# Turning gathered expert rows without TensorE: store, permuting loads and VectorE transposes, in a fused attention and mixture-of-experts kernel

## Chip, cores and metric

The kernel runs on one core of one Trainium2 chip. The metric is device time in microseconds (us). Before the change the median of 3 runs is 1353.02 us (1351.83 to 1355.73).

## The reference

The input x is 8 x 1024 rows of 256. Every row is layer-normalised; on the result xn two branches run, and the output is x + attention(xn) + experts(xn) + xn.

```python
Q, K, V = heads(xn @ Wq + bq), heads(xn @ Wk + bk), heads(xn @ Wv + bv)   # 16 heads of 16
Qp = relu(Q / |Q| @ projection) + 0.1          # 64 features per head; Kp the same from K
KV, K_sum = Kp^T V, sum over the sequence of Kp
out = (Qp KV) / max(Qp K_sum, 1e-6) @ Wo + bo

logits = xn @ router_w.T ; probs = softmax ; top 2 of 8 experts, weights renormalised
rank = position of the pair in its expert's list ; keep = rank < 2561
h = silu(rows of expert e @ w1[e])             # 256 -> 1024
y = h @ w2[e]                                  # 1024 -> 256
combined = sum over the two experts of weight * y
```

## The kernel before, in words

float32 products are made from float16 halves (high, low): each product is three matmul passes, high x high, high x low, low x high. `hl` in names means such a pair.

**Attention and routing.** Eight batches, each of 1024 rows in two halves of four 128-row tiles. A turn (`dve_turn`, `act_turn`, `pe_turn`, `pool_turn`, `sp_turn`) lists by hand, for each engine, its work on batch b and on the preparation of batch b+1, in order; engines meet by semaphores. Eight PSUM banks: four `big`, three `small` used in a ring, and a side bank. The steps that the change touches:
- `xn_high` (ScalarE) rounds half a batch of xn to float16, `x_low` (GpSimd, line 1038) takes the remainder, `x_transpose` (TensorE) turns both. `xhl` is also stored to DRAM as `xn_split`, 512 float16 per row (high 256, low 256).
- `q_relu` (ScalarE, line 522) and `q_low` (VectorE, 1369) split the query features; `kv_build` (VectorE) makes the kv matrix, with the cast of line 1360.
- The constant 0.1 of the features is handled apart. `constant_part` (VectorE, line 1378) writes norm x cn, for a 128-row tile 16 heads x 17 numbers, into `nd`; four tiles per half, so eight instructions per batch. `cn_b` is copied from PSUM by ScalarE. `attend_drain` (line 1385) adds the PSUM result of `attend` (TensorE, 823) to it.
- `norms` (VectorE) makes the norms of half 0, `norm_refine` (GpSimd) those of half 1.
- `place` finds each pair's slot, and `scatter` (GpSimd, line 1078) writes the batch's slot-table records to DRAM in 16 indirect DMAs. The batch before last still has 13 of them left when the tail begins; the last batch's 16 follow.

**Experts.** `tile_table` lists 71 tiles: the first 64 (`PT`) have 256 rows (two blocks of 128), the last 7 have one block, each tile of one expert. Per tile t:
- GpSimd: `meta_load` (1158) reads row numbers and weights of the tile, `gather` (1166) fetches its rows from `xn_split`, one indirect DMA per block, three tiles ahead (`XR` = 4 buffers, `xg`), `add_out` (1173) adds the result rows to the output in DRAM.
- TensorE: `hidden` (962) makes 1024 x rows in 48 matmuls, then `rows_turn` of tile t+1 (946: four transposes of 128 x 128 per block into bank 0 or 1), then `expert_out` of tile t-1 (979, 24 matmuls per block).
- VectorE: `hidden_split` splits silu(h) (1549, 1551, four times), then `rows_copy` of tile t+1 (1540) copies the turned rows from PSUM to `moe_xT`, then for the first 28 tiles `w_low` makes a low half of the next expert's weights (1263).
- ScalarE: silu (629), `w_high`, and `y_scale` (639).
- SP: in its order, for each tile, it waits for `rows_turned` and issues one `w_load` of 512 KB (tiles 1 to 26; line 410). Before the tiles it issued the output stores of the last batch.

The experts' SBUF area overlays attention's. VectorE therefore waits for the last output stores before its first `rows_copy` (line 1627).

## Time and profile before

| | |
|---|---|
| median of 3 runs | 1353.02 us (1351.83 to 1355.73) |
| profiled execution | 1353.69 us, span 1352.1 us |
| TensorE matmul (PE) busy | 1201.2 us, 89% |
| TensorE weight load (PEld) | 972.5 us, 72%, beside the matmuls |
| VectorE (DVE) | 870.9 us, 64% |
| GpSimd (POOL) | 679.7 us, 50% |
| ScalarE (ACT) | 621.4 us, 46% |
| `expert_out`, line 979 | 3240 matmuls, 365.3 us |
| `hidden`, line 962 | 3408 matmuls, 376.7 us |
| `rows_turn`, line 946 | 540 transposes |
| `rows_copy`, line 1540 | 71 copies, 0.68 us of a two-block tile |
| `constant_part`, line 1378 | 64 products, 433 ns |
| DMA | 80.64 MB, mean 60 GB/s |
| SP's DMA queue (q1) | 39330 packets, 9.5% of 16 engines |
| GpSimd's DMA queue (q0) | 32288 packets, 17.1% |

Shares are of the whole span, over two stages of very different kind: attention and routing until about 585 us, the experts after it. A matmul's busy time includes its latency, so that of single groups adds up to more than the time they occupy; the chain of waits gives the share of the path. "Idle before" is the time an engine did nothing before an instruction, with what released it; "issue" means that nothing in the profile shows a releaser. A DMA's "landing" is the time from its issue to its last byte.

### The profile page before, as it was taken

The numbers are of one execution on the slowest core, as the hardware profiler recorded it, in microseconds if no ns is written. First come the engines' busy times: TensorE is split into PE (matmuls) and PEld (weight loads), VectorE is DVE, ScalarE is ACT, GpSimd is POOL, SyncE is SP. The second block draws the span as 40 slices with busy tenths as digits, with TensorE's granted clock in tenths as the row PEclk, the third lists the DMA queues.
The fourth block names the chain that finished last, engine by engine and source line by source line (L and its number), as shares of the span: only waits on it lengthen the run. The fifth ranks groups of instructions, "written<-read, shape, count | busy, mean of one in ns | idle before, by whom it ended". The sixth has DMA issues, their size and how long they took to land.

```text
span 1352.1 us, 38635 instructions
## 1 busy us (share of the span) xinstructions
PE 1201.2 (89%) x14708; PEld 972.5 (72%) x14708; DVE 870.9 (64%) x2024; ACT 621.4 (46%) x1101; POOL 679.7 (50%) x646
## 2 busy tenths in 40 slices
PE   3779787878787888379999999999999999999997
PEld 1446464646564556259999999999999999989986
DVE  6778989898988886845555555554444444444442
ACT  3476767676757676333333333332222233233322
POOL 3313363636463637735555555555555555555542
PEclk9889798979888989589999999999999999999999
DMA  4111212112121111034444444433232332233330
GB/s 139 55 39 38 75 42 71 62 52 66 49 64 33 34 33 34 2 98 91 107 100 95 95 95 96 82 50 52 49 52 46 49 48 48 48 50 50 46 44 7
DMA packets 71788, 80.64 MB, mean 60 GB/s; under 512 B 14817, under 2 KB 65250, under 8 KB 71618
## 3 DMA queue, kind: packets, MB, share of 16 engines
q0 software_dynamic: 32288, 34.78, 17.1%
q1 hardware_dynamic: 39330, 43.39, 9.5%
q8 instruction: 131, 2.15, 0.7%
q14 instruction: 39, 0.32, 0.1%
HBM read 44.13 MB, written 34.92 MB: 58 GB/s over the span
## 4 chain that ended last, share of the span: by engine, by line
PE 66%; DVE 20%; issue 5%; ACT 4%; POOL 3%; DMA 1%; DVEq 0%; SPq 0%; ACTq 0%; POOLq 0%
PE bank L962 27%; PE bank L979 26%; DVE area L1369 4%; PE bank L703 2%; PE bank L823 2%; PE bank L946 2%; DVE area L1229 1%; PE bank L792 1%; DVE area L1378 1%; ACT area L502 1%; PE bank L809 1%; PE bank L764 1%; DVE area L1271 1%; DVE area L1360 1%; DVE area L1300 1%
## 5 line engine op out<-in xcount | busy, mean ns | idle before, releaser
L962 PE MATMUL bank<-area 128*128 128x256 f16 (+1 forms) x3408 | 376.7, 269 | 5.7 <-issue 3.1
L979 PE MATMUL bank<-area 128*128 x3240 | 365.3, 273 | 0.0
L962 PEld LDWEIGHTS bank<-area 128*128 x3408 | 324.7, 98 | 48.0 <-issue 7.8
L1549 DVE TENSOR_SCALAR area<-area 128x512 f16<-128x512 f32 (+1 forms) x284 | 125.3, 441 | 353.9 <-ACT area L629 350.7
L1173 POOL DMA_INDIRECT out_dram<-area,mt x135 | 218.4, 1618 | 247.4 <-ACT area L639 207.8
L979 PEld LDWEIGHTS bank<-area 128*128 128x128 f16 x3240 | 313.7, 98 | 35.6
L629 ACT ACTIVATE area<-bank 128x512 f32<-128x512 f32 (+1 forms) x284 | 163.7, 577 | 185.7 <-PE bank L962 184.2
L1078 POOL DMA_INDIRECT slot_table<-area x128 | 136.5, 1067 | 153.9 <-PE bank L823 96.7
L639 ACT ACTIVATE area<-bank,mt 128x256 f32<-128x256 f32 x135 | 57.1, 471 | 317.5 <-PE bank L979 317.5
L1551 DVE SCALAR_TENSOR_TENSOR area<-area 128x512 f16<-128x512 f32 (+1 forms) x284 | 189.5, 667 | 9.8
L1166 POOL DMA_INDIRECT xg<-xn_split,mt x135 | 135.4, 1003 | 42.6 <-issue 40.2
L703 PE MATMUL bank<-area,w_hl 128*128 128x512 f16 x384 | 91.5, 397 | 1.3 <-ACT area L540 1.3
L1158 POOL DMA_DIRECT2D mt<-slot_table x71 | 52.8, 743 | 77.3 <-issue 77.3
L522 ACT ACTIVATE area<-bank 128x512 f16<-128x512 f32 x128 | 67.4, 603 | 39.7 <-PE bank L809 19.8
L1369 DVE SCALAR_TENSOR_TENSOR area<-bank,area 128x512 f16<-128x512 f32 x128 | 79.6, 682 | 9.2 <-ACT area L522 8.4
L703 PEld LDWEIGHTS bank<-area,w_hl 128*128 128x128 f16 x384 | 38.1, 102 | 47.7 <-issue 9.8
L809 PE MATMUL bank<-area,p_hl 32*128 32x512 f16 x384 | 47.1, 429 | 27.8 <-DVE area L1369 24.6
L823 PEld LDWEIGHTS bank<-area 128*128 128x128 f16 x1536 | 44.2, 104 | 31.2 <-issue 23.8
L1038 POOL TENSOR_TENSOR area<-area 128x1024 f16<-128x1024 f32 x16 | 34.9, 2182 | 60.1 <-ACT area L534 60.1
L823 PE MATMUL bank<-area 128*128 128x34 f16 x1536 | 46.4, 188 | 20.7 <-issue 16.3
L728 PE MATMUL bank<-w_hl,area 128*128 128x264 f16 x384 | 51.8, 280 | 12.6 <-DVE area L1412 6.7
L728 PEld LDWEIGHTS bank<-w_hl,area 128*128 128x128 f16 x384 | 35.4, 99 | 37.4 <-DVE area L1412 14.2
(195 smaller groups left out, 1485.4 us busy)
## 6 DMA issues: line engine op xcount, KB each, us to landing
w_raw<-in_w_dram SPq DMA_DIRECT2D x18, 512.0 KB, 4.4
area<-in_x_dram SPq DMA_DIRECT2D x16, 512.0 KB, 5.9
xn_split<-area SPq DMA_DIRECT2D x16, 512.0 KB, 2.9
out_dram<-area SPq DMA_DIRECT2D x32, 256.0 KB, 3.5
area<-in_w_dram SPq DMA_DIRECT2D x14, 512.0 KB, 4.6
xg<-xn_split,mt POOLq DMA_INDIRECT x135, 3.4
out_dram<-area,mt POOLq DMA_INDIRECT x135, 3.9
slot_table<-area POOLq DMA_INDIRECT x128, 2.8
```

The source lines that it names most:

```text
L629: nc.scalar.activation(h32[j].rearrange("p a b -> p (a b)")[:, 0:n], big[j][:, 0:n], ACT.Silu, scale=1.0 / R_SCALE).then_inc(mh_silu, 1)
L703: mm = nc.tensor.matmul(big[n][:, :], w_hl[:, wl, k, c0:c0 + P], xT[half][:, xl * KC + k, :], start=(i == 0 and k == 0), stop=(i == 2 and ...
L728: mm = nc.tensor.matmul(dst[:, 0:D + E], xT[half][:, xl * KC + k, tl * P:(tl + 1) * P], w_hl[:, wl, k, 2 * D:], start=(i == 0 and k == 0), ...
L823: mm = nc.tensor.matmul(dst[:, p_ * KVW:(p_ + 1) * KVW], rq[:, p_, rl, tl * P:(tl + 1) * P], kv_hl[:, kl, p_, :], start=(i == 0), stop=(i ...
L962: mm = nc.tensor.matmul(big[j][:, i2 * n:(i2 + 1) * n], we[:, bass.ds(e * EXPERT + (k * 2048 + wl * 1024 + c * P), P)], moe_xT[t % XT][:, ...
L979: mm = nc.tensor.matmul(yb[:, a * D:(a + 1) * D], hT[u % 2][:, c, hl, a * P:(a + 1) * P], we[:, bass.ds(e * EXPERT + off, D)], start=(c == ...
L1078: nc.gpsimd.indirect_dma_start(meta, bass.IndirectOffsetOnAxis(slot_i[b % 2][:, k, t:t + 1], 0), rec[b % 2][:, k, t, :], None).then_inc(me ...
L1166: nc.gpsimd.indirect_dma_start(xg[:, t % XR, a, :], None, xs, bass.IndirectOffsetOnAxis(mt[:, u % GRP, a, 0:1], 0)).then_inc(rows_in[t % X ...
L1173: nc.gpsimd.indirect_dma_start(orows, bass.IndirectOffsetOnAxis(mt[:, u % GRP, a, 0:1], 0), y_sb[u % 2][:, a, :], None, bounds_check=last_ ...
L1369: v.scalar_tensor_tensor(rq[:, p_, 1, :], big[n % BIG_BANKS][:, :], 0.0, rq[:, p_, 0, :], ALU.max, ALU.subtract).then_inc(qf_split, 1)
L1549: v.tensor_scalar(hi, h, H_SCALE, None, ALU.mult).then_inc(mh_step, 1)
L1551: v.scalar_tensor_tensor(lo, h, H_SCALE, hi, ALU.mult, ALU.subtract).then_inc(mh_split, 1)
```

## The change

Two parts, and two moves that go with them.

1. The gathered rows of an expert tile are no longer turned by TensorE. SP stores them from `xg` to a DRAM buffer (`rows_keep`), loads them back in eight DMAs that permute runs of 64 float16 (`rows_move`), so that every 32 x 32 block lies where its transpose belongs, and VectorE transposes all blocks in one instruction from `xq` to `moe_xT` (`rows_turn`). `xq` has three buffers in the place of `w_hl`. The rows of w1 are loaded in an order that matches (four DMAs of 32 partitions in place of one). `gather` runs four tiles ahead, `meta_load` five.
2. `constant_part` moves from VectorE to GpSimd, after `x_low` of each half; in the tail before `scatter`. `attend_drain` waits for it at the first tile of each half (`const_ready`), and GpSimd waits for the norms of half 0 (`norms_set`).
3. In `act_turn` `xn_high` of half 0 moves behind the first four `q_relu` and the copy of vsum, that of half 1 behind the last four `q_relu`.

```diff
--- before.py
+++ after.py
@@ -287,6 +295,7 @@
         dump_i = oh.bitcast(I32)[:, :, 0, :]
 
 
+        xq = w_hl.rearrange("p a b c -> p (a b c)")[:, 0:XQ * 2 * QUAD * P].rearrange("p (r b a n) -> p r b a n", r=XQ, b=2, a=QUAD)
         we = area[:, 0:E * EXPERT // 2].bitcast(F16)
         cursor[0] = E * EXPERT // 2
         moe_xT = [view([2 * KC, TS], F16) for _ in range(XT)]
...
@@ -397,17 +409,18 @@
         def w_load(sp, e, c):
 
             raw = w_raw[c % 2 if e == 0 else c]
-            if c < 2:
-                src = w1_rows[bass.ds(e * D + c * P, P), :]
-                dst = raw
-            else:
-                src = w2_rows[bass.ds(e * FF + (c - 2) * 4 * P, 4 * P), :].rearrange("(c p) d -> p c d", p=P)
-                dst = raw.rearrange("p (c d) -> p c d", c=4)
+            loaded = w_in[c % 2 if e == 0 else c]
             if e == 0 and c >= 2 or e == 1 and c < 2:
                 hold(sp, w_lo, e * 4 + c - 1)
             elif e > 1:
                 hold(sp, w_lo, e * 4 + c - 3)
-            sp.dma_start(dst, src).then_inc(w_in[c % 2 if e == 0 else c], 16)
+            if c < 2:
+                for q in range(QUAD):
+                    sp.dma_start(raw[32 * q:32 * q + 32, :],
+                                 w1_rows[bass.ds(e * D + (q * KC + c) * 32, 32), :]).then_inc(loaded, 16)
+            else:
+                src = w2_rows[bass.ds(e * FF + (c - 2) * 4 * P, 4 * P), :].rearrange("(c p) d -> p c d", p=P)
+                sp.dma_start(raw.rearrange("p (c d) -> p c d", c=4), src).then_inc(loaded, 16)
 
         def x_load(sp, b, half):
 
...
@@ -443,6 +456,25 @@
             out_store(sp, b, 3)
             if b < 4:
                 w_load(sp, (b + 2) // 4, (b + 2) % 4)
+
+        def rows_keep(sp, t):
+
+            sp.wait_ge(rows_in[t % XR], ring(t))
+            n = blocks(t)
+            sp.dma_start(turn[bass.ds(t % XR * TS, n * P), :].rearrange("(b p) n -> p b n", p=P),
+                         xg[:, t % XR, 0:n, :]).then_inc(rows_kept[t % 2], 16)
+
+        def rows_move(sp, t):
+
+            sp.wait_ge(rows_kept[t % 2], 16 * (t // 2 + 1))
+            if t >= XQ:
+                sp.wait_ge(rows_turned, t - XQ + 1)
+            n = blocks(t)
+            src = turn[bass.ds(t % XR * TS, n * P), :].rearrange("(m i) (h c n) -> c h i m n", i=32, h=2, c=QUAD)
+            for c in range(QUAD):
+                dst = xq[32 * c:32 * c + 32, t % XQ, 0:n, :, :].rearrange("i b a (h n) -> i (b a) h n", h=2)
+                for h in range(2):
+                    sp.dma_start(dst[:, :, h, :], src[c, h]).then_inc(rows_moved[t % XQ], 16)
 
         @block.sync
         def _(sp):
...
@@ -482,16 +514,18 @@
 
             sp_turn(sp, B - 1, "tail")
             for t in range(MT):
+                rows_keep(sp, t)
                 if t > 0:
-                    sp.wait_ge(rows_turned, t)
+                    rows_move(sp, t - 1)
                 if 1 <= t < 4 * (E - 1) - 1:
                     w_load(sp, (t + 1) // 4 + 1, (t + 1) % 4)
+            rows_move(sp, MT - 1)
 
 
         def w_high(act, e, c):
 
             raw = c % 2 if e == 0 else c
-            hold(act, w_in[raw], (c // 2 + 1 if e == 0 else e + 2 if c < 2 else e) * 16)
+            hold(act, w_in[raw], ((QUAD + c // 2) if e == 0 else QUAD * (e + 1) + 1 if c < 2 else e) * 16)
             nc.scalar.activation(we_parts[:, e, c, 0, :], w_raw[raw], ACT.Copy, scale=R_SCALE).then_inc(w_hi, 1)
 
         def qk_read_half(act, b, half, n0=0, n1=4):
...
@@ -581,8 +613,10 @@
             nc.scalar.copy(cs_b.rearrange("p h d -> p (h d)"), take(act, phase, "attn", "vsum", b)[:, 0:H * (HD + 1)]) \
                 .then_inc(attn_taken, 1)
             if body:
+                xn_high(act, b + 1, 0)
+            q_relu(act, b, 0, 4, PAIRS)
+            if body:
                 xn_high(act, b + 1, 1)
-            q_relu(act, b, 0, 4, PAIRS)
             nc.scalar.copy(cn_b.rearrange("p h d -> p (h d)"), take(act, phase, "attn", "cn", b)[:, 0:H * (HD + 1)]) \
                 .then_inc(attn_taken, 1)
             if body:
...
@@ -935,22 +969,11 @@
             v_project(pe, phase, b + 1, HT + 3)
             k_features(pe, b + 1, 1)
 
-        def rows_turn(pe, t):
-
-            pe.wait_ge(rows_in[t % XR], ring(t))
-            if t > 1:
-                pe.wait_ge(rows_ready, t - 1)
-            dst = f16(bank[t % 2]).rearrange("p (h n) -> p h n", h=2 * KC)
-            for a in range(blocks(t)):
-                for h in range(2 * KC):
-                    mm = nc.tensor.transpose(dst[:, h, a * P:(a + 1) * P], xg[:, t % XR, a, h * P:(h + 1) * P], ident16[:, :])
-            mm.then_inc(rows_turned, 1)
-
         def hidden(pe, t, u, first):
 
             e = pe.value_load(tab[0:1, 0, bass.ds(t, 1)], min_val=0, max_val=E - 1)
             hold(pe, w_lo, e * 4 + 4)
-            pe.wait_ge(rows_ready, t + 1)
+            pe.wait_ge(rows_turned, t + 1)
             n = blocks(t) * P
             for j in range(4):
                 if not first:
...
@@ -1069,6 +1089,17 @@
             link(g.tensor_tensor(nu, nsq, ny, ALU.mult), apart=True)
             g.tensor_scalar(norm[:, half], nu, 1e-8 * W_SCALE, None, ALU.add).then_inc(norm_ready, 1)
 
+        def constant_part(pool, b, half):
+
+            wait_read(pool, "attn", "cn", b)
+            if b > 0:
+                pool.wait_ge(o_split, b * 2 - 1 + half)
+            pool.wait_ge(norms_set, b + 1)
+            for t in range(HT):
+                ins = nc.gpsimd.tensor_tensor(nd[half][:, t], norm[:, half, t, 0:2, :].rearrange("p g e -> p (g e)").unsqueeze(2)
+                                              .broadcast_to([P, H, HD + 1]), cn_b, ALU.mult)
+            ins.then_inc(const_ready, 1)
+
         def scatter(pool, b, n0, n1):
 
             if n0 == 0:
...
@@ -1080,10 +1111,13 @@
 
         def pool_turn(pool, b, phase):
             if phase == "tail":
+                for half in range(2):
+                    constant_part(pool, b, half)
                 scatter(pool, b, 0, TOPK * NT)
                 return
             for half in range(2):
                 x_low(pool, b + 1, half)
+                constant_part(pool, b, half)
             if b > 0:
                 pool.wait_ge(attn_filled, nth("attn", f"ab{NT - 2}", b))
                 scatter(pool, b - 1, 0, 5)
...
@@ -1159,8 +1193,8 @@
 
             def gather(t, u):
                 if t >= XR:
-                    pool.wait_ge(rows_turned, t - XR + 1)
-                if t >= 4:
+                    pool.wait_ge(rows_kept[t % 2], 16 * ((t - XR) // 2 + 1))
+                if t >= 5:
                     hold(pool, meta_in, t * 16 + 16)
                 for a in range(blocks(t)):
                     nc.gpsimd.indirect_dma_start(xg[:, t % XR, a, :], None, xs,
...
@@ -1177,21 +1211,21 @@
             def group(g, first=False, last=False):
                 for u in range(LASTG if last else GRP):
                     t = g * GRP + u
-                    if not (last and u >= LASTG - 3):
-                        gather(t + 3, u + 3)
+                    if t + 4 < MT:
+                        gather(t + 4, u + 4)
                     if not (first and u == 0):
                         hold(pool, added, 16 * done(t))
-                    if not (last and u >= LASTG - 4):
-                        meta_load(t + 4, u + 4)
+                    if t + 5 < MT:
+                        meta_load(t + 5, u + 5)
                     if first and u == 0:
                         for n in range(2):
                             pool.wait_ge(out_stored[n], 16 * 2 * B)
                     add_out(t, u)
 
+            for t in range(5):
+                meta_load(t, t)
+            pool.wait_ge(meta_in, 16 * 5)
             for t in range(4):
-                meta_load(t, t)
-            pool.wait_ge(meta_in, 16 * 4)
-            for t in range(3):
                 gather(t, t)
             group(0, first=True)
             for g in range(1, NG - 1):
...
@@ -1286,7 +1320,8 @@
                          v.scalar_tensor_tensor(nu, nu, -0.5, ny, ALU.mult, ALU.mult))
                 chp.link(v.scalar_tensor_tensor(ny, ny, 1.5, nu, ALU.add, ALU.mult) if step == 2 else
                          v.scalar_tensor_tensor(ny, nu, 1.5, ny, ALU.add, ALU.mult))
-            chp.link(v.tensor_scalar(norm[:, 0], ny, 1e-8 * W_SCALE, None, ALU.add))
+            v.tensor_scalar(norm[:, 0], ny, 1e-8 * W_SCALE, None, ALU.add).then_inc(norms_set, 1)
+            dve.wait_ge(norms_set, b + 1)
 
         def v_over_norm(dve, b, half, ch):
             ts = slice(half * HT, (half + 1) * HT)
...
@@ -1427,12 +1453,10 @@
             if not body:
                 place(dve, b, first)
                 tile_table(dve)
-            constant_part(dve, b, 0)
             for t in range(HT - 1):
                 attend_drain(dve, phase, b, t)
             if not body:
                 table_read(dve, phase, b)
-            constant_part(dve, b, 1)
             attend_drain(dve, phase, b, HT - 1)
             q_low(dve, b, 1, 0, 4)
             q_low(dve, b, 1, 4, PAIRS)
...
@@ -1531,14 +1555,14 @@
             src = drain(dve, phase, "attn", "tab", b)[0:1, 0:2 * P].rearrange("p (k t) -> p k t", k=2)
             v.tensor_copy(tab[:, :, :], src[:, :, 0:MT]).then_inc(attn_read, 1)
 
-        def rows_copy(dve, t):
-
-            dve.wait_ge(rows_turned, t + 1)
+        def rows_turn(dve, t):
+
+            dve.wait_ge(rows_moved[t % XQ], moved(t))
             if t >= XT:
                 dve.wait_ge(mh_filled, (t - XT) * 4 + 4)
-            n = blocks(t) * P
-            v.tensor_copy(moe_xT[t % XT][:, :, 0:n], f16(bank[t % 2]).rearrange("p (h n) -> p h n", h=2 * KC)[:, :, 0:n]) \
-                .then_inc(rows_ready, 1)
+            n = blocks(t)
+            v.transpose(moe_xT[t % XT][:, :, 0:n * P].rearrange("p h (m i) -> p h m i", i=32),
+                        xq[:, t % XQ, 0:n, :, :].rearrange("p b a (h j) -> p h (b a) j", j=32)).then_inc(rows_turned, 1)
 
         def hidden_split(dve, t, u):
             for j in range(4):
```

The calls of `constant_part` in `dve_turn` and of TensorE's `rows_turn` in `group` go, and VectorE's `group` calls the new `rows_turn` where it called `rows_copy`.

## Rows read from the trace of the kernel before

**Rows 1.** Stretches: length, then busy us of PE, PEld, DVE, ACT, POOL, clock, DMA.

```profile
300.00:400.00 100.00, 83.50 (x1422) 57.50 (x1421) 88.50 (x258) 67.63 (x120) 57.23 (x63) 0.94 0.19 60
700.00:800.00 100.00, 100.00 (x954) 90.03 (x952) 57.10 (x91) 38.57 (x66) 55.05 (x46) 1.00 0.46 96
1000.00:1100.00 100.00, 100.00 (x956) 90.07 (x954) 48.22 (x85) 29.50 (x55) 55.41 (x47) 1.00 0.31 51
```

**Rows 2.** Chain of waits, expert tiles near the end: start us, us, what.

```profile
1272.96 0.45 PE bank L946 x8
1273.40 5.24 PE bank L979 x48
1278.64 5.24 PE bank L962 x48
...
1304.54 4.29 PE bank L962 x48
```

**Rows 3.** Timeline, first expert tiles: start us, us, instruction, [idle before it].

```profile
584.02 0.99 POOL L1166 DMA_INDIRECT xg<-xn_split,mt  x1 [0.30 <-issue]
...
586.56 0.95 POOL L1166 DMA_INDIRECT xg<-xn_split,mt  x1 [0.30 <-issue]
...
589.28 0.69 DVE L1540 COPY area<-bank 128x1024 f16<-128x1024 f16 x1 [3.31 <-DMA out_dram<-area]
```

**Rows 4.** Instructions of one line: min/median/max ns, first and last start.

```profile
L1263 DVE SCALAR_TENSOR_TENSOR area<-w_raw,area x18: 1206/1212/2289, 130.9 to 871.0; 128x1024 f16<-128x1024 f32 x18
...
L1047 POOL TENSOR_TENSOR area<-area x8: 725/1160/1598, 59.0 to 533.0; 128x256 f32<-128x256 f32 x8
...
L1378 DVE TENSOR_TENSOR area<-area x64: 420/433/442, 80.9 to 555.8; 128x272 f32<-128x272 f32 x64
...
L1360 DVE CAST area<-area x8: 516/1958/1959, 75.8 to 539.6; 128x272 f16<-128x272 f32 x8
```

**Rows 5.** Timeline of one expert tile.

```profile
1005.31 5.40 PE L962 MATMUL bank<-area 128*128 128x256 f16 x48
...
1006.63 1.67 POOL L1173 DMA_INDIRECT out_dram<-area,mt  x1 [3.14 <-ACT area L639]
...
1011.82 0.98 POOL L1166 DMA_INDIRECT xg<-xn_split,mt  x1 [0.30 <-issue]
1011.85 0.70 DVE L1551 SCALAR_TENSOR_TENSOR area<-area 128x512 f16<-128x512 f32 x1
```

**Rows 6.** SP DMA queue: packets, MB, share; whole span, then 9-10 us.

```profile
q1 hardware_dynamic: 39330, 43.39, 9.5%
...
q1 hardware_dynamic: 286, 0.03, 22.2%
```

**Rows 7.** DMA issues, us to landing last: 1000-1100, 700-800, whole span.

```profile
xg<-xn_split,mt POOLq DMA_INDIRECT x20, 2.8
...
xg<-xn_split,mt POOLq DMA_INDIRECT x18, 4.4
...
area<-in_proj_t_dram SPq DMA_DIRECT2D x8, 8.0 KB, 2.8
```

**Rows 8.** Timeline of SP's issues at the start.

```profile
6.42 3.73 SPq L463 DMA_DIRECT2D area<-in_proj_t_dram  x8
```

**Rows 9.** Chain of waits, first two expert tiles.

```profile
590.23 8.15 PE bank L962 x48
...
598.82 2.18 issue
```

**Rows 10.** Timeline of GpSimd, end of attention.

```profile
553.28 0.97 POOL L1078 DMA_INDIRECT slot_table<-area  x1 [1.73 <-issue]
...
576.69 0.79 POOL L1158 DMA_DIRECT2D mt<-slot_table  x1 [3.31 <-issue]
```

**Rows 11.** Timeline of one batch of attention.

```profile
208.62 2.12 POOL L1038 TENSOR_TENSOR area<-area 128x1024 f16<-128x1024 f32 x1 [1.15 <-ACT area L534]
208.94 1.96 DVE L1360 CAST area<-area 128x272 f16<-128x272 f32 x1
```

More of the change, by code:

```diff
@@ L21 @@
 KC = D // P
+QUAD = P // 32
 PAIRS = H // 2
@@ L37 @@
 XT = 4
+XQ = 3
 NG = -(-MT // GRP)
@@ L45, in blocks, with moved @@
     return 2 if t < PT else 1
+def moved(t):
+    return 16 * 2 * QUAD * (t // XQ + 1)
 def done(t):
@@ L160, in moe_attention @@
     xs = nc.dram_tensor("xn_split", [N + P, 2 * D], F16, kind="Internal").ap()
+    turn = nc.dram_tensor("turned_rows", [XR * TS, 2 * D], F16, kind="Internal").ap()
     meta = nc.dram_tensor("slot_table", [META_ROWS, 2], I32, kind="Internal").ap()
@@ L338, in moe_attention @@
         kv_split = sem("kv_split")
+        const_ready, norms_set = sem("const_ready"), sem("norms_set")
         masks_ready = sem("masks_ready")
@@ L352, in moe_attention @@
         rows_in = [sem(f"rows_in{i}") for i in range(XR)]
-        rows_turned, rows_ready = sem("rows_turned"), sem("rows_ready")
+        rows_kept = [sem(f"rows_kept{i}") for i in range(2)]
+        rows_moved = [sem(f"rows_moved{i}") for i in range(XQ)]
+        rows_turned = sem("rows_turned")
         mh_filled, mh_silu = sem("mh_filled"), sem("mh_silu")
@@ L574, in act_turn @@
             k_relu(act, b, 3)
-            if body:
-                xn_high(act, b + 1, 0)
             act.wait_ge(gate_in, b + 1)
@@ L1025, in group @@
                 return e
-            rows_turn(pe, 0)
             expert = group(0, None, first=True)
@@ L1370, in q_low @@
                                        ALU.max, ALU.subtract).then_inc(qf_split, 1)
-        def constant_part(dve, b, half):
-            wait_read(dve, "attn", "cn", b)
-            if b > 0:
-                dve.wait_ge(o_split, b * 2 - 1 + half)
-            for t in range(HT):
-                ins = v.tensor_tensor(nd[half][:, t], norm[:, half, t, 0:2, :].rearrange("p g e -> p (g e)").unsqueeze(2)
-                                      .broadcast_to([P, H, HD + 1]), cn_b, ALU.mult)
-                cha.step(ins)
-            cha.wait()
         def attend_drain(dve, phase, b, t):
+            if t % HT == 0:
+                dve.wait_ge(const_ready, b * 2 + t // HT + 1)
             src = drain(dve, phase, "attn", f"ab{t}", b)[:, 0:H * (HD + 1)].rearrange("p (h d) -> p h d", h=H)
@@ L1627, in _ @@
                 dve.wait_ge(xs_stored[n], 16 * B)
-            rows_copy(dve, 0)
+            rows_turn(dve, 0)
             for g in range(NG - 1):
```

4 lines of the change are left out of this document (1 added, 3 removed).

## The prediction

> **What bounds the kernel now.** I read the busy shares by stretch first [rows 1]. Two programs follow each other. From 300 to 400 us (attention and routing) VectorE is busy 88.5 of 100 us and TensorE 83.5: many short waits, VectorE nearest to the bound. From 700 us on (experts) TensorE is busy 100.00 of 100, VectorE 57 and later 48, GpSimd 55, and the DMA share is 0.46 while weights stream in and 0.31 after that. So an expert tile costs what TensorE's instructions cost. The chain of waits confirms it [rows 2]: per tile of 256 rows 5.24 us for the 48 matmuls of `hidden`, 0.45 us for the 8 transposes, 5.24 us for the 48 of `expert_out`, nothing between: 10.93 us.
>
> **Transposes leave TensorE.** 64 tiles have two blocks (8 transposes) and 7 have one (4), together 540. Eight cost 0.45 us [rows 2], 0.056 each. Tile 0's lie before the first expert matmul, tile 1's inside a stall priced below. The other 62 two-block tiles give 62 x 0.45 = 27.9 us, the seven one-block tiles 7 x 0.22 = 1.6. Together **-29.5 us**, if nothing else becomes late. A tile is then 10.48 us.
>
> **Does the new path hold 10.48 us per tile?** Three resources:
> - VectorE. The copy of 0.69 us [rows 3] becomes a transpose of the same 1024 elements. No row shows one: it is bounded by that copy from below and by the 1.21 us of a two-operand pass over 1024 elements [rows 4] above (2.29 once). I take 1.2, since a transpose can hardly beat a copy. `hidden` of the tile ends at 1005.31 + 5.24 = 1010.55 [rows 5], the last split at 1011.85 + 0.70 = 1012.55 [rows 5]; the turn ends at 1013.8, and the next `hidden` wants it at 1010.55 + 5.24 = 1015.8. Slack 2.0 us; even 2.3 us would still fit (0.9 left). Behind the turn wait the low halves of the weights and the next splits, due a half tile later. Cost 0.
> - DMA engines. Eight loads of 256 runs of 128 B are 2048 packets per tile, the store 256 of 1 KB. The nearest short packets are the 64-float rows of `proj_t` and the single floats of the biases: 286 packets took 22.2% of 16 engines in 1 us [rows 6], 12.4 ns each. 2048 x 12.4 / 16 = 1.6 us. Over the whole span a packet of SP's queue (1.1 KB) took 0.095 x 16 x 1352.1 / 39330 = 52 ns [rows 6], so the store adds 0.8 us. 2.4 us of 10.48 is 0.23 on top of 0.46 or 0.31: 0.7 at most. The upper bound, 52 ns for short packets too, is a rival below. I take 12.4: the size is nearer.
> - Latency, because SP is in order: `rows_keep(t)` stands ahead of `rows_move(t-1)`, so tile t-1 moves only when the gather of t has landed. Measured from the end of `expert_out(t-5)` (1005.3): the two adds start at 1006.63 and the second gather at 1011.82 [rows 5], +6.5. Its landing takes 2.8 us, 4.4 while weights load [rows 7]: +9.3 or +10.9. The store's issue and eight load issues at 3.73 / 8 = 0.47 each [rows 8] put the last load at +13.1 or +14.7, its landing 2.8 us later [rows 7], the turn 1.2: +17.1 or +18.7. `hidden(t-1)` is due after four half tiles, +21.0. Slack 3.9, or 2.3 while weights load. Cost 0, but this is the thinnest cover of the change. SP's other work per tile (w1 in four issues instead of one, 1.4 us more) fits: 5.6 us of 10.48. One-block tiles: the chain loses the second add and gather (-3.2 us: 13.9), while two tiles last 2 x (4.29 [rows 2] + 2.62) = 13.8: about even, cost 0 to 5.
>
> The Trainium skill, "DMA: Bandwidth & Descriptors" (Specifications), puts line rate at 512 B and more and calls smaller transfers read-modify-write; its rules for kernel authors warn of a plain DMA with a rearranged pattern as a transpose (19 times slower). The second does not apply, as each run stays 128 B long; by the first the short packets would cost like long ones, which is the DMA rival below. The 12.4 ns speak against it.
>
> **The start of the experts, +15.3 us.** This is the term that takes back half of the gain. It has two parts, both in the chain to the first `hidden`, which now starts at 590.23 [rows 9].
> - GpSimd. In the last batch `constant_part` of both halves stands before `scatter`. GpSimd is not free there: the scatters of the batch before end at 553.28 - 1.73 = 551.55, the last sixteen follow, then the table reads at 576.69 [rows 10] and the gathers. Eight products of 272 elements: the nearest GpSimd row is 256 elements, 0.725 to 1.6 us, median 1.16 [rows 4]; the 0.725 was in the tail, beside short VectorE operations, and I scale it to 0.8. 8 x 0.8 = 6.4 us, of which the 1.73 us of idle may or may not be kept: +5.5 (4.7 to 12). A fifth table read before the first gather: 0.79 and a gap, +1.2. So the second gather of tile 0 starts at 584.02 [rows 3] + 6.7 = 590.7 and lands 3.3 later (between the 2.8 and 4.4 of [rows 7]), 594.0.
> - The detour. Store: issue 0.5 and a landing of 3.1, between the 2.8 and 4.4 of the gathers [rows 7]: 597.6. The gathers of tile 1 (586.56 [rows 3] + 6.7 + 3.3 = 596.6), which `rows_keep(1)` awaits, are in by then. Eight issues: the last at 600.9, landed 603.7. Turn: 604.9. `hidden(0)` at 605.0: +14.8.
> - `hidden(0)` itself took 8.15 us for 48 matmuls [rows 9], 2.9 more than at full speed. TensorE idles longer before it now; I expect the same 8.15 (bounds: 0, and the doubling of all 48, +2.3). Then `hidden(1)` waited 2.18 us more for the copy [rows 9]; the turn is 0.5 longer: +0.5.
>
> **Attention: -4 us.** VectorE loses 8 products of 0.433 us [rows 4] per batch, 28 us in all, but most of it was beside something. The second half's four end just as ScalarE, behind `attend(3)`, delivers the first relu. The first half's four become GpSimd's 4 x 0.8 = 3.2 us behind the same copy of cn, so the drains begin about when they do now. In the last batch they start only at 551.55 and cost 0.5 us on VectorE's path, which is covered by the chain above. What does shorten the chain is the cast of kv: it lasts 1.96 us in seven batches and 0.52 in the tail [rows 4]; it starts at 208.94, in the middle of GpSimd's `x_low` at 208.62 (2.12 us), and ends with it [rows 11]. With `xn_high` moved behind four relus and a copy, `x_low(0)` starts about 207.4 (an estimate) and is off the cast in batches whose TensorE is early (four of seven): up to 1.4 us each, about 1.0 after the drains' new wait. Four times 1.0 = 4. Bounds: the other way, if GpSimd's products take 1.16, each drain starts 1.4 late, +0.6 per batch (+4); all the VectorE time, -24, I exclude down to -12, as `attend(3)` and the relus remain.
>
> **Sum.** -29.5 + 15.3 - 4 = -18.2, on the profiled execution's 1353.7 us (span 1352.1): 1335.5. The median of the runs is 1353.0, 0.7 below it: **1335 us**.
>
> **Rivals.**
> - *Late rows (15%), slower.* If the last of the eight loads lands later than 19.8 us after `expert_out(t-5)` ends, TensorE stalls in every tile. Against: 15.9 to 17.5 worked out. For: the landings of 2.8 were of 8 KB loads on a quiet queue, the gather needs 4.4 beside weights, and SP may need longer per issue. At 1 us per tile over all 62 tiles the price is +62: 1397; in the 27 tiles with weight loads alone +27: 1362. It decides from 0.3 us per tile, where the gain of 18 is gone.
> - *DMA engines full (10%), slower.* At 52 ns for every packet a tile asks 2048 x 52 / 16 + 0.8 = 7.5 us, beside 0.46 x 10.48 = 4.8: 12.3 us against 10.48 in 27 tiles (+50), and 10.7 in the others (+9): 1335 + 59 = 1394.
> - *A dearer start (8%), no change.* GpSimd's products at 1.16 (+3), slower landings and TensorE's slow stretch lengthened: start 25, attention +3: -29.5 + 25 + 3 = -1.5: 1352.
> - *Attention gives more (20%).* The cast is free in all seven batches and the drains start earlier: -12, start 12: -29.5: 1324.
>
> **Numbers.** Forecast 47%, own range 1328 to 1342. A measurement of this kernel tells from no change about 0.3%, 4 us. Faster by more: 47 + 20 + a small part of late rows, 0.70. Within: 0.08. Slower: 0.22. The range holds the forecast, the better attention and the nearer half of late rows: 1321 to 1364.
>
> **What would show it.** Tiles of 10.48 us after 650 us and no idle of `hidden` on VectorE's turn (right), or a wait on the loads there (late rows); DMA share of 0.55 to 0.7, not above 0.9; the turn at 0.7 to 1.3 us; GpSimd's products at 0.8 and the first table read near 582; first `hidden` near 601 (605 less attention's 4); the kv cast near 0.5 us in some batches. The forecast is wrong if the first `hidden` is later than 610, or tiles are longer than 10.7.

## The result and the profile after

The changed kernel takes 1345.85 us (median of 6 runs, 1341.41 to 1348.42), the kernel before beside it 1353.45 us (6 runs, 1351.37 to 1356.2): ratio 0.9943, 95% interval 0.9928 to 0.9958. The gain is 7.6 us where 18 were forecast. The changed kernel's profiled execution took 1348.42 us (span 1346.8); it is the slowest of the six, so the profiled spans differ by 5.3 us where the medians differ by 7.6.

The page's busy times and three of its groups: line, engine, operation, tiles and count, then busy us, mean ns, idle time before and what ended it. Line 985 is `hidden`, 1564 VectorE's `rows_turn`.

```profile
PE 1178.7 (88%) x14168; PEld 947.0 (70%) x14168; DVE 885.4 (66%) x1960; ACT 621.9 (46%) x1101; POOL 724.8 (54%) x710
q1 hardware_dynamic: 205842, 78.83, 23.2%
L985 PE MATMUL bank<-area 128*128 128x256 f16 (+1 forms) x3408 | 378.8, 271 | 31.1 <-DVE area L1564 22.2
L1564 DVE STREAM_TRANSPOSE area<-w_hl 128x1024 f16<-128x1024 f16 (+1 forms) x71 | 84.3, 1187 | 47.6 <-DMA w_hl<-turned_rows 47.5
```

TensorE lost 540 transposes, but `hidden` now idles behind the turn, and the turn behind its loads. Of the 22.2 us put down to the turn, 18.0 are the wait of the very first tile; the other two waits, 2.3 and 1.9 us, are among the one-block tiles. The stretches, as in [rows 1], tell where the rest of the time goes:

```profile
300.00:400.00 100.00, 84.22 (x1523) 58.36 (x1521) 83.59 (x253) 66.76 (x121) 57.45 (x67) 0.91 0.19 60
700.00:800.00 100.00, 97.62 (x890) 86.39 (x888) 63.16 (x92) 38.60 (x65) 58.12 (x47) 1.00 0.72 146
1000.00:1100.00 100.00, 100.00 (x919) 89.63 (x917) 53.72 (x84) 29.97 (x57) 56.10 (x48) 1.00 0.56 102
```

In attention VectorE is busy 83.6 of 100 us where it was 88.5. From 1000 us TensorE is full and a tile lasts 10.48 us, as forecast; from 700 to 800 us, while weights load, it idles 2.4%. What ended the waits from 640 to 900 us (us in total, times, longest; line 1564 is the turn, 985 `hidden`):

```profile
DVE area L1564 <- DMA w_hl<-turned_rows: 25.0, 17, 3.0
PEld bank L985 <- issue: 6.7, 7, 1.3
PE bank L985 <- issue: 4.8, 7, 1.1
```

One of those stalls, in the timeline. Line 1200 is a gather, 464 the store `rows_keep`, 477 the loads `rows_move`, 419 a w1 load:

```profile
733.21 0.99 POOL L1200 DMA_INDIRECT xg<-xn_split,mt  x1 [0.30 <-issue]
...
738.70 0.38 SPq L464 DMA_DIRECT2D turned_rows<-xg  x1
739.18 4.08 SPq L477 DMA_DIRECT2D w_hl<-turned_rows  x8
...
743.31 2.81 SPq L419 DMA_DIRECT2D w_raw<-in_w_dram  x4
...
747.41 1.25 DVE L1564 STREAM_TRANSPOSE area<-w_hl 128x1024 f16<-128x1024 f16 x1 [3.03 <-DMA w_hl<-turned_rows]
...
748.86 5.43 PE L985 MATMUL bank<-area 128*128 128x256 f16 x48 [1.06 <-issue]
```

The second gather lands 5.5 us after its start; only then does SP store that tile and, behind the store, load the tile before. The eighth load is issued from 742.7 to 743.3 and is there at 747.4. The profile names no releaser for the 1.06 us of `hidden`, but the turn ends at 748.66, 0.2 us before `hidden` starts.

The profiled spans, split at three starts of `hidden` (before, after, and their difference):

| | before | after | |
|---|---|---|---|
| start of tile 2 | 612.0 | 620.7 | +8.7 |
| tile 2 to tile 64 (62 tiles) | 677.2 | 655.9 | -21.3 |
| tile 64 (first of one block) to the end | 62.9 | 70.2 | +7.3 |

62 x 10.48 is 649.8, so the middle holds 6.1 us of stalls, all before 900 us. The end, in the chain of waits (first column start, then us): the row of a one-block tile passes addition, table read, gather, store and loads, and `hidden` waits.

```profile
1279.93 5.44 PE bank L1002 x48
...
1288.46 4.07 DMA out_dram<-area,mt
...
1293.80 4.19 DMA mt<-slot_table
...
1298.77 3.66 DMA xg<-xn_split,mt
...
1302.44 0.34 SPq L464
...
1307.34 2.65 DMA w_hl<-turned_rows
...
1310.01 0.72 DVE area L1564
...
1310.92 4.76 PE bank L985 x48
```

From the end of that `expert_out` (1285.4) to `hidden` at 1310.9 the chain takes 25.5 us, while TensorE has three one-block tiles to do, 20.7 us: it waits 4.8 us, in three pieces. The table read stands in the chain because GpSimd, in its order, waits for the landing of the additions before it reads the table of a later tile.

And 3.5 us lie where no view shows an instruction. GpSimd's last addition, before and after:

```profile
1345.71 1.56 POOL L1173 DMA_INDIRECT out_dram<-area,mt  x1 [1.41 <-DMA out_dram<-area,mt]
```

```profile
1336.93 1.55 POOL L1207 DMA_INDIRECT out_dram<-area,mt  x1 [1.46 <-DMA out_dram<-area,mt]
```

It ends 4.8 us before the end of the span of 1352.1, but 8.3 us before that of 1346.8. In the raw records of the trace GpSimd's last instruction, a drain that the kernel doesn't write, lasts 3219 ns before and 6690 ns after.

### The profile page after: what moved, and what is told of

Read it like the earlier page. It is cut to its first block, busy times and chain, and to the rows that moved or that the text cites. A ratio compares the mean times of both kernels' runs of the same rounds, so it can differ in the third digit from the quotient of the medians.

```text
span 1346.8 us, 38196 instructions
## 1 busy us (share of the span) xinstructions
PE 1178.7 (88%) x14168; PEld 947.0 (70%) x14168; DVE 885.4 (66%) x1960; ACT 621.9 (46%) x1101; POOL 724.8 (54%) x710
## 4 chain that ended last, share of the span: by engine, by line
PE 52%; DMA 2%; issue 2%; POOL 1%; SPq 1%; POOLq 0%; DVE 0%; ACT 0%; DVEq 0%
PE bank L985 27%; PE bank L1002 26%; POOL slot_table L1109 1%; SPq L477 1%; DMA xg<-xn_split,mt 1%; DMA out_dram<-area,mt 1%; DMA mt<-slot_table 0%; DMA w_hl<-turned_rows 0%; POOL xg L1200 0%; POOLq L1190 0%; POOL out_dram L1207 0%; DVE area L1564 0%; ACT area L673 0%; POOL mt L1192 0%; SPq L464 0%
## 5 line engine op out<-in xcount | busy, mean ns | idle before, releaser
L985 PE MATMUL bank<-area 128*128 128x256 f16 (+1 forms) x3408 | 378.8, 271 | 31.1 <-DVE area L1564 22.2
L1207 POOL DMA_INDIRECT out_dram<-area,mt x135 | 222.8, 1650 | 220.6 <-ACT area L673 189.6
L1564 DVE STREAM_TRANSPOSE area<-w_hl 128x1024 f16<-128x1024 f16 (+1 forms) x71 | 84.3, 1187 | 47.6 <-DMA w_hl<-turned_rows 47.5
L556 ACT ACTIVATE area<-bank 128x512 f16<-128x512 f32 x128 | 67.8, 601 | 56.9 <-PE bank L843 39.1
L843 PE MATMUL bank<-area,p_hl 32*128 32x512 f16 x384 | 49.9, 446 | 23.4 <-DVE area L1404 20.1
```

Source lines behind the costliest of these rows:

```text
L985: mm = nc.tensor.matmul(big[j][:, i2 * n:(i2 + 1) * n], we[:, bass.ds(e * EXPERT + (k * 2048 + wl * 1024 + c * P), P)], moe_xT[t % XT][:, ...
L1207: nc.gpsimd.indirect_dma_start(orows, bass.IndirectOffsetOnAxis(mt[:, u % GRP, a, 0:1], 0), y_sb[u % 2][:, a, :], None, bounds_check=last_ ...
L1564: v.transpose(moe_xT[t % XT][:, :, 0:n * P].rearrange("p h (m i) -> p h m i", i=32), xq[:, t % XQ, 0:n, :, :].rearrange("p b a (h j) -> p ...
```

## Experiments

Ratios are to the kernel before, run beside each set on one chip. In the first set (attention only, rows only, loads first, small weight loads) the kernel before took 1396.79 us: there attention was some 28 to 39 us later in every kernel, taken at the last batch's vsum (last section), and the chain to the first `hidden` ran through attention's last output store, not through GpSimd. From tile 2 on the expert stage ran as on the other chips. So ratios and stretches are compared, not times.

**The changed kernel again** (second set)

> The changed kernel itself, beside the others on their chip. [...] Theory: stretches of the expert stage are the same on any chip, so again about 6 us of stalls between the third tile and tile 64, about 5 us among the one-block tiles, and 8.3 us between the last instruction and the end of the span, where the kernel before has 4.8; ratio to before 0.993 to 0.996. Rival: the stalls are an accident of the first profile; then the ratio is that of the order experiment, 0.986.

1348.01 us, ratio 0.9942 (0.9921 to 0.9963). Tile 2 to 64: 657.8 us, so 8.1 us of stalls; the end 68.6; the drain 6690 ns. The rival fell: stalls and drain belong to the kernel.

**Attention part only**, run in the first set and again in the third

```diff
                 x_low(pool, b + 1, half)
+                constant_part(pool, b, half)
...
-            constant_part(dve, b, 0)
             for t in range(HT - 1):
                 attend_drain(dve, phase, b, t)
...
-            constant_part(dve, b, 1)
```

> The kernel before with parts 2 and 3 of the change alone: constant_part on GpSimd, xn_high later; TensorE still turns the rows. My theory: attention gains 4 to 6 us by its last batch, and GpSimd's eight products before the last scatters (5.0 us) give nearly all of it back at the start of the experts, because the chain to the first expert tile runs through GpSimd. First hidden near 589, total 1350 to 1354. Rival (attention's gain reaches the end): the first hidden starts 5 us or more earlier than before, total 1346 to 1348, and then most of the measured gain of 7.6 us is this part's and the row path gives almost nothing.

> The attention-only experiment once more, on a chip that feeds TensorE its instructions without the stall seen in the first set, if this is one. Theory: vsum of the last batch 4 to 6 us earlier than before, last scatters 4 earlier less the 5.0 us of products before them: first hidden within 1 us of before, total within 2 us of it, ratio 0.998 to 1.001. Rival: 4 us of gain reach the end, ratio 0.997.

First set: 1394.31 us, ratio 0.9996 (0.9964 to 1.0028). Third set: 1348.67 us, 0.9963 (0.9949 to 0.9976), -5.0 us, and the first `hidden` at 585.2 us against 590.2 [rows 9]. There the rival was right: attention's gain reaches the end. The two intervals overlap, so the sets don't contradict each other. The chain says why: before, it ran through the last output store (586.00, 2.99 us) to VectorE's first copy [rows 3]; now it runs through GpSimd's last scatters and gathers:

```profile
575.47 2.59 DMA mt<-slot_table
...
578.34 1.03 POOL xg L1181
...
579.67 3.72 DMA xg<-xn_split,mt
...
584.27 0.70 DVE area L1545
...
585.21 6.75 PE bank L963 x48
```

The last batch's vsum starts at 527.80 us against 535.81, 8.0 us earlier; `hidden` only 5.0. GpSimd had little room at the end of attention: before, the rows were turned 1.4 us ahead of the copy at 589.28 [rows 3]. Its eight products (4.87 us here) used up that and a part of the gain, of which the run with the last products on VectorE, below, gets 3.1 us back.

**Only the later xn_high** (fourth set)

```diff
             k_relu(act, b, 3)
-            if body:
-                xn_high(act, b + 1, 0)
...
             if body:
+                xn_high(act, b + 1, 0)
+            q_relu(act, b, 0, 4, PAIRS)
+            if body:
                 xn_high(act, b + 1, 1)
-            q_relu(act, b, 0, 4, PAIRS)
```

> The kernel before with only the later xn_high on ScalarE (part 3); constant_part stays on VectorE. Theory of the forecast: the move frees the cast of kv from GpSimd's x_low in about half of the batches (cast of 14.2 us in all, 9 to 10 expected) and brings most of attention's gain: ratio 0.996 to 0.998, vsum of the last batch 4 us earlier. Rival: the gain is VectorE's 28 us of products gone; then this kernel is within 0.1% of before, whatever the cast does, or slower, since GpSimd's and ScalarE's later work holds the next batch.

1352.32 us, ratio 0.9991 (0.9977 to 1.0005), vsum of the last batch at 536.01 us (535.81 before). The kv cast did get shorter; before, and here:

```profile
L1360 DVE CAST area<-area 128x272 f16<-128x272 f32 x8 | 14.2, 1778 | 0.3
```

```profile
L1360 DVE CAST area<-area 128x272 f16<-128x272 f32 x8 | 8.4, 1046 | 0.3
```

5.8 us off that cast brought nothing measurable (the interval allows up to 3 us). The two attention kernels differ in the products alone, and only the one that has them off VectorE gains. The other profiles of the second to fourth set and of the result agree: the last vsum starts at 534.4 to 536.4 us in the five kernels with the products on VectorE and at 522.6 to 529.7 in the seven with them on GpSimd. The products without the later `xn_high` were not run.

**Rows only** (first set): the changed kernel with `constant_part` and `xn_high` as before.

> The changed kernel with parts 2 and 3 undone: the new row path alone. My theory: the tiles give -21 us, the detour before the first tile costs about 10, the end costs about 7, so a gain of 2 to 4 us: 1349 to 1351. Rival (the row path carries all of the gain, parts 2 and 3 are neutral or a loss): 1344 to 1346. If the products on GpSimd delay the start by their full 5.0 us and attention gives nothing, this kernel is faster than the changed one, 1341.

1392.51 us, ratio 0.9966 (0.9940 to 0.9992), between theory and rival. Middle 657.7, end 69.0 us, drain 6690 ns: the stalls and the longer drain come with the row path.

**Loads first** (first set)

```diff
             for t in range(MT):
-                rows_keep(sp, t)
                 if t > 0:
                     rows_move(sp, t - 1)
+                rows_keep(sp, t)
```

> The changed kernel with one order altered: SP issues the eight loads of tile t-1 before it waits for the gather of tile t. Theory (SP's order): the stalls between 620 and 870 us (6.1 us in all) and those among the one-block tiles (about 7 us) come because the loads of t-1 stand behind the gather of t, which itself waits for additions to the output; with the order altered the loads go out a few us earlier, both stalls shrink to under 2 us each, and tile 0 moves about 3 us sooner: total 1331 to 1336. Rival (full DMA engines while weights load): the stalls in the weight stretch stay at 5 to 6 us, only the end gains: 1338 to 1343. Second rival (what is late is the gather itself, through additions and buffers): no change, 1345.

1377.09 us, ratio 0.9863 (0.9824 to 0.9901): 0.8% below the changed kernel's 0.9942 (from the second set; it was not run in this one). Middle 649.8 us, that is 62 x 10.48 with no stall; end 65.6. From 700 us on with weights loading, at a DMA share higher than in the changed kernel:

```profile
700.00:800.00 100.00, 100.00 (x919) 89.63 (x917) 66.08 (x96) 39.20 (x66) 57.46 (x48) 1.00 0.74 149
```

So full DMA engines are out as the cause, and the order is it. SP's queue in this kernel:

```profile
747.05 0.38 SPq L464 DMA_DIRECT2D turned_rows<-xg  x1
...
749.36 3.86 SPq L477 DMA_DIRECT2D w_hl<-turned_rows  x8
```

The loads of a tile follow its own store by 2.3 us; in the changed kernel they followed the next tile's store, one tile of 10.5 us later. Whether tile 0 moved sooner, as the theory had it, can't be read in this set: SP's last output store was issued at 617.92, and the first store of rows stands behind it in the same order.

**Small weight loads** (first set)

```diff
-                    sp.dma_start(raw[32 * q:32 * q + 32, :],
-                                 w1_rows[bass.ds(e * D + (q * KC + c) * 32, 32), :]).then_inc(loaded, 16)
+                    k = 8 if e > 1 else 1024
+                    sp.dma_start(raw[32 * q:32 * q + 32, 0:k],
+                                 w1_rows[bass.ds(e * D + (q * KC + c) * 32, 32), 0:k]).then_inc(loaded, 16)
...
```

> The changed kernel with the weight loads of experts 2 to 7 cut to 8 columns each (it leaves out the loading of these weights; the number of issues stays). Theory (contention): landings between 620 and 870 us fall to those of the later tiles and the 6.1 us of stalls go: 1339 to 1341, tiles of 10.48 from the third on. Rival (SP's own issue time for the four loads of w1 makes the rows late): the issues stay, so at least 4 of the 6.1 us stay: 1343 to 1345. The end is not touched by either: its 7 us stay.

1381.70 us, ratio 0.9882 (0.9846 to 0.9917). Middle 649.8 us, no stall, though the issues are as many; end 69.2, untouched. So it is the bytes of the weight loads, which make gathers and loads land later, not SP's issue time, that used up the room. Order and traffic are both needed for the stall: taking away either one removes it. At the end there is no weight traffic and the order alone is left: 69.2 here, 65.6 with the loads first.

**Last constant_part on VectorE** (second set): the tail's eight products back before its drains.

> The changed kernel with the last batch's constant_part back on VectorE, before its drains, so that GpSimd goes from one batch's scatters straight to the next. Theory: the products held up the last sixteen scatters by 5.0 us, so first hidden 4 to 5 us earlier than in the changed kernel beside it, where GpSimd is busy without a gap into the last scatters; where GpSimd waits there anyway for the placing by VectorE, 0 to 1 us. Rival: VectorE's 3.5 us of products delay the placing or the output stores and it is 1 to 3 us slower.

1343.28 us, ratio 0.9920 (0.9903 to 0.9937). First `hidden` at 594.8 us, 3.1 us earlier than in the changed kernel beside it (597.9): theory, at somewhat less than its price. In time the two kernels differ by 4.7 us; the intervals of their ratios overlap.

**Ghost DMAs** (second set) and **ghost DMAs with more semaphores** (third): the kernel before, with the change's store and eight loads per tile to a buffer that nobody reads.

```diff
+                    sp.dma_start(turn[0:n * P, :].rearrange("(b p) n -> p b n", p=P),
+                                 wo_hl.rearrange("p a b c -> p (a b c)")[:, 0:n * 2 * D].rearrange("p (b n) -> p b n", b=n)).then_inc(ghost_kept, 16)
+                    src = xs[0:n * P, :].rearrange("(m i) (h c n) -> c h i m n", i=32, h=2, c=4)
...
+                            sp.dma_start(dst[:, :, h, :], src[c, h]).then_inc(ghost_moved, 16)
```

> The kernel before with the same store and eight permuting loads per tile issued by SP to a buffer that nobody uses; TensorE turns the rows as before. Theory: the traffic itself slows nothing in the steady tiles, which stay at 10.93 us, so 0 to 2 us there, and it adds the 3.5 us after the last instruction if these come from SP's many DMAs: 1.0025 to 1.004 times before. Rivals: contention on the DMA engines makes gathers late and stalls TensorE in the weight stretch by 3 us or more (1.005 and up); or the 3.5 us come from the changed program rather than its DMAs, and the span ends 4.8 us after the last instruction.

> The ghost kernel with six more semaphores than the kernel before, as many as the change adds, in the place of two; the same DMAs. Theory: the 8.3 us between GpSimd's last instruction and the end of the span, against 4.8 in the kernel before and in the ghost kernel with two more, is the clearing of the semaphores that the program uses: 8.3 here. Rival: it comes from something else of the changed program (its code, VectorE's transpose, another last instruction): 4.8 here.

1355.47 us, ratio 1.0013 (1.0001 to 1.0024), and 1356.16 us, 1.0016 (1.0006 to 1.0026). TensorE stays full in the weight stretch; the row is of the first of them:

```profile
700.00:800.00 100.00, 100.00 (x954) 90.05 (x953) 57.27 (x91) 37.56 (x63) 54.82 (x46) 1.00 0.74 149
```

The middle stays 677.2 us in both, the drain 3219 ns. The traffic costs the old kernel about 2 us, around the start (tile 2 at 614.9 and 613.5 against 612.0), and lengthens no drain; nor do six more semaphores. Both theories on the end fell. These loads read `xn_split` and wait for no gather, so the two runs price the traffic and not the order.

**First two tiles on TensorE**, with the loads first (second set)

```diff
+            for h in range(2 * KC):       # rows_first_turn, tiles 0 and 1, per block
+                for q in range(QUAD):
+                    n0 = (h // KC * QUAD + q) * KC * 32 + h % KC * 32
+                    transpose(dst[32*q:32*q+32, h, ...], xg[:, t % XR, a, n0:n0+32])
```

> The changed kernel with the altered order (loads of t-1 before the gather of t) and the rows of tiles 0 and 1 turned by TensorE (32 small transposes per block, straight from the gathered buffer) and copied by VectorE, as before the change. Theory: the detour before the first tile (store, eight loads, turn: from 585.5 to 598.1 us in the changed kernel) shrinks to 3 us, so the third tile starts 8 to 10 us earlier: 8 us less than the order experiment, ratio to before 0.979 to 0.982. Rival: tile 2's rows then come last, and TensorE waits for them: 2 to 4 us gained only.

1326.57 us, ratio 0.9792 (0.9774 to 0.9810), as the theory had it. The first tile now:

```profile
585.43 1.04 PE L984 MATMUL bank<-ident,xg 128*32 128x128 f16 x32 [4.80 <-DMA xg<-xn_split,mt]
586.63 0.69 DVE L1583 COPY area<-bank 128x1024 f16<-128x1024 f16 x1 [5.27 <-PE bank L984]
587.57 7.50 PE L1000 MATMUL bank<-area 128*128 128x256 f16 x48 [1.09 <-DVE area L1583]
```

2.1 us from the landed gather to `hidden`, where the changed kernel needed 12.6, from its store's issue at 585.48 to 598.08. Tile 2 starts at 609.9, 11.1 us earlier than in the changed kernel beside it.

**Both, and the tail on VectorE** (third set), and **the same path without attention's part** (third).

> The order altered, the first two tiles turned by TensorE, and the last batch's constant_part on VectorE, together. Theory: the chain to the first tile runs through GpSimd's last scatters, so the 3.1 us that the tail experiment won at the first hidden add up with the other gains: first hidden near 584.5, 2 to 4 us less than the first-two-tiles experiment (1326.6), about 1323. Rival: with the detour gone, VectorE's chain to the output stores and the first copy is as late as GpSimd's, the 3.5 us of products are then on the path, and it is 0 to 2 us slower: 1326 to 1329.

> The first-two-tiles kernel (altered order too) without parts 2 and 3 of the change: constant_part on VectorE in every batch, xn_high in its old places. Theory: parts 2 and 3 bring 4 us at the last batch and cost 3 at GpSimd's last scatters, so here the time is 0 to 2 us longer: 1327 to 1329. Rival: attention's gain reaches the end in full, and this kernel is 4 us or more slower, 1331 and up.

1323.56 us, ratio 0.9775 (0.9760 to 0.9790), first `hidden` at 585.1: theory. Without attention's part, which puts the last products on VectorE as well, 1330.30 us, 0.9828 (0.9815 to 0.9841), between its two cases: attention's part is worth 6.7 us in the same set, with the tail's products on VectorE. With them on GpSimd the comparison is with another set, 3.7 us by the times and 4.9 by the ratios.

**Three tiles ahead** (fourth set): the kernel of ratio 0.9775 with

```diff
-                    if t + 4 < MT:
-                        gather(t + 4, u + 4)
+                    if t + 3 < MT:
+                        gather(t + 3, u + 3)      # meta_load one less ahead too
```

> The best kernel so far (order altered, first two tiles by TensorE, last constant_part on VectorE; 1323.6 us) with gathers three tiles ahead and table reads four, as before the change, instead of four and five. Theory on the end of the span: GpSimd's last wait for its own queue (3.2 us before, 6.7 us after the change) grows with how far its gathers run ahead of its additions, so it is 3.2 us here, and the start is one table read (1.2 us) earlier. Rival: it comes from the row path as such, and stays 6.7 us. On the tiles: the chain from a gather to its use has 10.5 us less room; theory: the altered order leaves too little, and TensorE stalls by 3 us or more per tile, 1400 us and up; rival: the room of the fourth tile wasn't needed, tiles stay at 10.48 and the total is 1319 to 1322.

1326.11 us, ratio 0.9791 (0.9768 to 0.9813), not distinguishable from 0.9775. The drain is 3219 ns again: its length goes with how far GpSimd's reads run ahead. In exchange the turns wait:

```profile
DVE area L1602 <- DMA w_hl<-turned_rows: 80.2, 60, 4.2
PE bank L1000 <- DVE area L1602: 6.3, 3, 3.8
PE bank L1000 <- issue: 2.1, 4, 1.4
```

From tile 2 to 64 that costs 3.4 us in all (653.2 against 649.8), nearly all of it while weights load, and not the 3 us per tile of the theory; from tile 64 to the end it is 67.8 us against 65.7 with four ahead, although the drain is 3.5 us shorter, so 5.5 us of stalls. The rival on the total fell too: the stalls, 8.9 us together, take more than the shorter drain and one table read less bring. The profiled execution (1320.96 us) is the fastest of its five and reached the first `hidden` at 577.0 us, 8.2 before the kernel with four ahead; but its last vsum was already 6.1 us earlier, where the two kernels do not differ, so only the stretches from tile 2 on are compared here.

## Why the prediction was wrong, step by step

- *Transposes leave TensorE, -29.5.* Right in size: the tile is 10.48 us, in all stretches without stalls.
- *VectorE's turn.* Taken at 1.2, measured 1.24. That is just above the upper of the two bounds, 1.21. The slack of 2.0 us held.
- *DMA engines.* 0.7 at most was forecast beside weights, 0.4 to 0.55 after; measured 0.72 and 0.56. From 1000 to 1100 us SP's 23047 packets took 24.3% of 16 engines, 16.9 ns each with a tenth of them 1 KB. In the raw records of that stretch a 128 B packet took 13.0 ns and a 1 KB packet 49.5: the 12.4 that I took for a short one was nearly right, though it was the mean of 162 packets of 4 B (9.0 ns) and 124 of 256 B (16.9). The rival of full engines (52 ns) is out. The Trainium skill, "DMA: Bandwidth & Descriptors" (Specifications), has its line rate from 512 B on; by it I had let short packets cost like long ones, 52 ns. The trace speaks against that reading, with 13.0 ns; it agrees with the Trainium skill in direction, since 128 B in 13.0 ns is half the rate of 1 KB in 49.5. No run here shows what a 512 B run would have cost.
- *Latency, cost 0.* **This step failed.** I called it the thinnest cover, worked out a slack of 2.3 us beside weights and charged nothing, with 2.8 us for the landing of the loads and 4.4 for the gather. Counted as there, from the start of an issue, they took 4.7 and, for the gather up to SP's store, 5.5 in the stall shown. The two landings, 1.9 and 1.1 longer, use up the 2.3 by themselves; the issues (0.2) and the step from the turn to `hidden` (0.2) make the rest of the 1.06 us. The new traffic is part of it: the median landing of a gather rose from 4.4 to 4.9 us beside weights (700 to 800 us) and from 2.8 to 3.3 without them (1000 to 1100 us) [rows 7]. That cost 6.1 us (8.1 in the second profile). The cause is the one that the step names, SP's order, and the experiment that turns it removes it whole. The rival *late rows* had the mechanism, but in a mild form: over the 27 tiles with weight loads 0.23 to 0.30 us each.
- *One-block tiles, 0 to 5, taken 0.* The end grew by 7.3 us: minus the 1.6 saved, 3.5 of drain, so 5.4 of stalls. This is above the bound by 0.4. **Here the path itself was wrong.** The chain of 13.9 us began at the additions just before the gather and left out the landing of the earlier additions and the table read behind it, 9.5 us from 1288.46 to the landing at 1297.99. The chain that bound took 25.5 us against 20.7 of TensorE's work.
- *The drain.* In no term: +3.5 us, which goes with gathers and table reads one tile further ahead. It could not be read from any row before.
- *Start of the experts, +15.3 with attention -4: first `hidden` at 601.* Measured 598.1; tile 2 came 8.7 us later than before, where 11.3 were forecast. GpSimd's eight products took 5.03 us and not 6.4. GpSimd reached the second gather at 582.42, forecast 590.7 less attention's 4; from there to `hidden` it took 15.7 us and not 14.3: the last load landed in 3.7 and not 2.8, the issues before it took 0.9 more than forecast, and gather and store 0.8 less. From the first `hidden` to tile 2 it is 22.6 us, 21.7 before; I had put the difference at 0.5.

```profile
542.91 5.03 POOL L1099 TENSOR_TENSOR area<-area 128x272 f32<-128x272 f32 x8
...
573.81 0.79 POOL L1192 DMA_DIRECT2D mt<-slot_table  x1 [3.98 <-issue]
...
588.56 4.68 SPq L477 DMA_DIRECT2D w_hl<-turned_rows  x8
...
596.58 1.25 DVE L1564 STREAM_TRANSPOSE area<-w_hl 128x1024 f16<-128x1024 f16 x1 [15.79 <-DMA w_hl<-turned_rows]
```

- *Attention, -4.* Size about right (-5.0 alone, -3.7 to -4.9 and -6.7 in the two other comparisons), reason wrong, so the size was luck. I gave it to the shorter cast and to the moved `xn_high`; that move alone brings 0.1%, inside its interval. What brings it is VectorE's time, of which I had written that most was beside something: at the last vsum the gain is 8.0 us, of which 5.0 reach the first `hidden`.

In sum, from the profiled spans: the forecast's -18.2, less 2.6 at the start, plus 6.1 of stalls beside weights, plus 8.9 at the end (5.4 of stalls, 3.5 of drain), and 0.5 in the middle (a tile saves 0.44 us, not 0.45), is the measured -5.3. The two covers that were thin and priced at zero, and one wait that no view lists, took the gain. The two covers are separable from the idea: the kernel of ratio 0.9775 keeps it without their stalls, with the 3.5 us of drain still in it, and reaches 1323.6 us. The drain alone was made short only by the kernel with three tiles ahead, which paid for it with stalls.

Open: what the drain waits for, and how it is tied to the distance of the reads. Why attention was later in the first set was not tested. Nor was the changed kernel itself run there, so that the two experiments on the stall are compared with it by stretches.

## What to carry over

A cover of 2 us that is a sum of DMA landings is not a cover: price it at its landings under the traffic of that stretch. In an in-order queue, put what is ready (loads of the tile already stored) before what waits (the store of the tile still arriving); here that order was worth a whole tile of room and 11 us. A chain is only worked out when it goes back to something that nothing else holds up: for the one-block tiles that was one addition and one table read further. A latency detour is worth having in steady state and not for the first tiles: start those on the short path.

## What the hardware showed unexpectedly

- GpSimd's closing drain: 3219 ns with gathers three tiles ahead, in seven profiles, and 6690 ns with four, in nine; nothing between.
- VectorE's transposing pass over 128 x 1024 float16 in blocks of 32 took 1.24 us, 0.70 for half, where the plain copy of 128 x 1024 from PSUM took 0.69 [rows 3].
- GpSimd's product of 272 elements took 0.65 us in the median (0.64 to 0.79), less than the shortest of its eight passes over 256, 0.725 [rows 4].
- A packet of 128 B in SP's queue took 13.0 ns of one DMA engine, one of 1 KB 49.5 ns (1000 to 1100 us of the changed kernel).
- On the first set's chip 64 small matmuls of the last batch that take 1.5 us in the kernel before took 18.3 (loads first), 15.4 (rows only) and 11.4 (attention only), in groups with gaps that nothing in the profile explains ("issue"). In the fourth profile of the set (small weight loads) they took 2.1, and attention was as late there. From the kernel with the loads first:

```profile
545.44 0.43 PE L826 MATMUL bank<-xg,area 128*32 128x64 f32 x4 [1.00 <-issue]
546.88 0.44 PE L826 MATMUL bank<-xg,area 128*32 128x64 f32 x3 [1.01 <-issue]
...
551.16 0.45 PE L826 MATMUL bank<-xg,area 128*32 128x64 f32 x3 [1.79 <-issue]
```

What held them back is not shown; no run tested it. By the fourth profile they are not all of the set's 28 to 39 us.
